# Three steps in fp32 products at the end of a sandwich kernel on one core, with the order behind the last scores written anew

## The reference

```python
def attn(x, weight_qkv, out_w, out_b):
    # q, k, v: a product whose low column bands are fp16, the middle band fp32
    q, k, v = split(mix_precision_matmul(x, weight_qkv))
    s = softmax(q / 16 @ k.T)
    return (s @ v) @ out_w.T + out_b

def ffn(x, W_r, W_k, W_v, mu_r, mu_k):
    x_prev = x shifted down by one row of its batch, zeros first
    xr = mu_r * x + (1 - mu_r) * x_prev
    xk = mu_k * x + (1 - mu_k) * x_prev
    r = sigmoid(xr @ W_r.T)
    k_act = relu(xk @ W_k.T) ** 2
    return r * (k_act @ W_v.T)

x = x + layernorm(attn(layernorm(x), ...))
x = x + layernorm(ffn(layernorm(x), ...))
```

## Time and profile before

| | |
|---|---|
| median of 3 runs | 807.6 us (807.54 to 808.79) |
| the profiled execution | 809.13 us, its span 807.3 us |
| TensorE busy | 784.2 us, 97% of the span |
| VectorE, ScalarE, POOL busy | 653.0 (81%), 576.7 (71%), 515.9 us (64%) |
| granted TensorE clock, mean | 0.993 |
| HBM read and written | 18.75 and 8.39 MB |

### The profile page before, as it was taken

The page is one execution under the profiler, slowest core; times in us unless marked ns, Lnnn a source line. Parts: engine busy times, 40 slices in busy tenths (PEclk is TensorE's granted clock), DMA queues, the critical chain, the costliest instruction groups (busy, mean ns, idle before and its releaser), DMA issues.

```text
span 807.3 us, 16567 instructions
## 1 busy us (share of the span) xinstructions
PE 784.2 (97%) x5839; PEld 574.0 (71%) x5839; DVE 653.0 (81%) x1681; ACT 576.7 (71%) x795; POOL 515.9 (64%) x752
## 2 busy tenths in 40 slices
PE   8999999999999999999999999999999999998983
PEld 6556777777777777777777777777777777777872
DVE  6788888877788979878888879978777788877876
ACT  4668668777777778877768687787767676675564
POOL 3340356765776868675676767876557657676674
PEclk9999999999999999999999999999999999999998
DMA  6788789577876768887666898857577766559301
GB/s 190 161 166 129 140 161 174 89 135 143 170 135 147 138 134 161 145 151 145 117 125 137 164 164 150 156 111 129 108 134 144 134 124 100 113 119 201 77 14 52
DMA packets 348243, 108.70 MB, mean 135 GB/s; under 512 B 321920, under 2 KB 347904, under 8 KB 348160
## 3 DMA queue, kind: packets, MB, share of 16 engines
q1 hardware_dynamic: 348160, 107.64, 69.6%
HBM read 18.75 MB, written 8.39 MB: 34 GB/s over the span
## 4 chain that ended last, share of the span: by engine, by line
PE 91%; DVE 3%; DMA 1%; issue 1%; POOL 1%; ACT 1%; POOLq 0%; DVEq 0%; ACTq 0%
PE Y L1492 7%; PE Y L1496 7%; PE Y L1493 7%; PE Y L1494 7%; PE Y L1495 7%; PE S L1471 7%; PE S L1475 7%; PE S L1474 7%; PE S L1473 7%; PE S L1472 7%; PE M L1436 6%; PE M L1438 6%; PE M L1437 6%; PE M L1453 1%; PE M L1451 1%
## 5 line engine op out<-in xcount | busy, mean ns | idle before, releaser
L1148 DVE TENSOR_SCALAR_CACHE_REDUCE probs<-S 128x512 f32<-128x512 f32 x256 | 172.9, 677 | 64.6 <-PE S L1475 64.4
L833 ACT ACTIVATE probs<-probs,exp_bias,kappa 128x2048 f32<-128x2048 f32 x64 | 133.9, 2092 | 64.2 <-DVE exp_bias L1161 64.2
L1166 DVE TENSOR_TENSOR p_lo<-probs,p_hi 128x2048 f16<-128x2048 f32 x62 | 171.5, 2767 | 7.3 <-ACT p_hi L762 7.3
L1493 PE MATMUL Y<-pt_lo,planes 128*128 128x256 f16 x496 | 135.2, 273 | 0.0
L1495 PE MATMUL Y<-pt_lo,planes 128*128 128x256 f16 x496 | 135.2, 273 | 0.0
L1494 PE MATMUL Y<-pt_hi,planes 128*128 128x256 f16 x496 | 135.2, 273 | 0.0
L1492 PE MATMUL Y<-pt_hi,planes 128*128 128x256 f16 x496 | 135.2, 273 | 0.0
L1496 PE MATMUL Y<-pt_hi,planes 128*128 128x256 f16 x496 | 135.2, 273 | 0.0
L762 ACT ACTIVATE p_hi<-probs 128x2048 f16<-128x2048 f32 x64 | 121.4, 1897 | 6.2 <-DMA pt_lo<-p_lo 6.1
L1471 PE MATMUL S<-turned,q_hi 128*128 128x512 f16 x256 | 97.1, 379 | 1.7 <-DVE probs L1148 0.9
L1475 PE MATMUL S<-turned,q_lo 128*128 128x512 f16 x256 | 97.0, 379 | 0.0
(11 more groups left out here) (223 smaller groups left out, 2032.6 us busy)
## 6 DMA issues: line engine op xcount, KB each, us to landing
x_res<-in_L_attn_x SPq DMA_DIRECT2D x32, 256.0 KB, 3.7
out_x<-gate SPq DMA_DIRECT2D x32, 256.0 KB, 3.2
xs<-in_L_attn_x SPq DMA_DIRECT2D x13, 512.0 KB, 4.7
pt_hi<-p_hi SPq DMA_TRANSPOSE x62, 5.0
pt_lo<-p_lo SPq DMA_TRANSPOSE x62, 4.8
xs<-in_L_attn_x SPq DMA_DIRECT2D x2, 256.0 KB, 4.0
gate<-in_L_attn_x SPq DMA_DIRECT2D x1, 512.0 KB, 6.8
att<-in_L_attn_x SPq DMA_DIRECT2D x1, 512.0 KB, 4.5
```

What stands on the lines that cost most here:

```text
L1148: dve.tensor_scalar(probs[:, h % 2, t, c * BLK:(c + 1) * BLK], S[k % RING][:, :], 1.0, None, ALU.mult, ALU.max, accum_out=chunk_max[:, t, ...
L1166: dve.tensor_tensor(p_lo[:, t, :], probs[:, h % 2, t, :], p_hi[:, t, :], ALU.subtract).then_inc(p_lo_made, 1)
L1493: pe.matmul(to[:, 0, :], low, p_l, start=False, stop=final, skip_group_check=True)
```

## The change

Steps 29, 30 and 31 (`h >= FULL`) no longer split. Their receptance, keys and feed are products of the fp32 tiles `mixed` and `square` with fp32 weights, which POOL makes once, in slots 218, 220 and 229, as the sum of the two planes (in tiles that batch 2 has left, `planes` and `turned`). An fp32 group is four products instead of 12. `split_high`, `split_low`, `sq_hi` and `squares_low` of these three steps are gone, and some waits name other semaphores (a mix of step 30 or 31 waits for the receptance or keys before it, no longer for the split). Behind the loop, the five lists by hand are in another order.

```diff
+    FULL = H - 3
+    FULL_AT = (218, 220, 229)
...
+        full = [f32(planes[:, 0].rearrange("p k l d -> p (k l d)")[:, NKT * ROWS:]).rearrange("p (w h c) -> p w h c", w=2, h=HALVES),
+                f32(turned[:, 0].rearrange("p k l d -> p (k l d)")[:, NKT * ROWS:]).rearrange("p (w h c) -> p w h c", w=2, h=HALVES)]
+        FULL_OF = {REC: full[0][:, 0], KEY: full[0][:, 1], VAL: full[1][:, 0]}
...
+            turn_low(H - 2, 1)
+            store(H - 8)
             turn_high(H - 2, 1)
-            turn_low(H - 2, 1)
-            load_residual(H - 3)
-            store(H - 8)
             turn_high(H - 1, 0)
...
+            def full_weight(w):
+                pool.wait_ge(pv_done, (NB - 1) * PER)
+                pool.tensor_tensor(FULL_OF[w], wt_hi[:, w], wt_lo[:, w], ALU.add).then_inc(full_made, 1)
...
             def squares(h):
                 act.wait_ge(key_done, h + 1)
-                if h >= LEFT:
+                if h > FULL:
+                    act.wait_ge(sq_made, h)
+                elif h >= LEFT:
                     act.wait_ge(sq_hi_made, h)
...
+                if h >= FULL:
+                    return
                 act.activation(sq_hi[:, :, :], relu[:, :, :], ACT.Square, scale=key_scale[:, 0:1]).then_inc(sq_hi_made, 1)
...
             def mix(h, i):
                 dve.wait_ge(diff_made, h + 1)
-                if h >= 1:
+                if h > FULL:
+                    dve.wait_ge(rec_done if i == 0 else key_done, h)
+                elif h >= 1:
                     dve.wait_ge(xm_lo_made[i], h)
...
+            def full_by_rows(to, a, w, done):
+                for t in range(RT):
+                    for e in range(HALVES):
+                        mm = pe.matmul(to[:, t * D:(t + 1) * D], a[:, e, t * P:(t + 1) * P], FULL_OF[w][:, e, :],
+                                       start=e == 0, stop=e == HALVES - 1)
+                mm.then_inc(done, 1)
...
             def receptance(h):
-                pe.wait_ge(xm_lo_made[0], h + 1)
+                if h >= FULL:
+                    pe.wait_ge(mixed_made[0], (h + 1) * HALVES)
+                    pe.wait_ge(full_made, 3)
+                else:
+                    pe.wait_ge(xm_lo_made[0], h + 1)
...
-            values(H - 3, 1, 2)
             project_out(H - 4, KEYS_LEFT)
-            values(H - 3, 2, 7)
+            values(H - 3, 1, 5)
+            mix_keys(H - 6, 0)
+            values(H - 3, 5, 8)
             receptance(H - 6)
             feed(H - 7)
             turn_mix_in(H - 5)
-            mix_keys(H - 6, 0)
-            values(H - 3, 7, 8)
             values(H - 2, 0, 3)
```

More of the change, by code:

```diff
@@ L483, in _ @@
             turn_low(H - 1, 1)
+            load_residual(H - 3)
+            store(H - 7)
             load_residual(H - 2)
-            store(H - 7)
+            load_residual(H - 1)
             store(H - 6)
-            load_residual(H - 1)
             store(H - 5)
@@ L1537, in receptance @@
                     pe.wait_ge(gated_made, h)
-                by_rows(REC_BANK, xm_hi[:, 0], xm_lo[:, 0], REC, rec_done)
+                if h >= FULL:
+                    full_by_rows(REC_BANK, mixed[:, 0], REC, rec_done)
+                else:
+                    by_rows(REC_BANK, xm_hi[:, 0], xm_lo[:, 0], REC, rec_done)
             def mix_keys(h, projects_begun):
-                pe.wait_ge(xm_lo_made[1], h + 1)
+                if h >= FULL:
+                    pe.wait_ge(mixed_made[1], (h + 1) * HALVES)
+                    pe.wait_ge(full_made, 3)
+                else:
+                    pe.wait_ge(xm_lo_made[1], h + 1)
                 if h >= KEYS_LEFT:
@@ L1548, in mix_keys @@
                     cols = slice(m * P, (m + 1) * P)
+                    if h >= FULL:
+                        for e in range(HALVES):
+                            mm = pe.matmul(pair(keys_bank(h)[:, :])[:, m, :], FULL_OF[KEY][:, e, cols], mixed[:, 1, e, :],
+                                           start=e == 0, stop=e == HALVES - 1)
+                        continue
                     for e in range(HALVES):
@@ L1560, in feed @@
                     pe.wait_ge(rec_made, h + 1)
-                by_rows(feed_bank(h), sq_hi, sq_lo, VAL, val_done)
+                if h >= FULL:
+                    full_by_rows(feed_bank(h), square, VAL, val_done)
+                else:
+                    by_rows(feed_bank(h), sq_hi, sq_lo, VAL, val_done)
             sources = [[stage_qkv[e][:, w * D:(w + 1) * D] for e in range(HALVES)] for w in range(3)]
@@ L1647, in _ @@
             turn_mix_in(H - 5)
-            mix_keys(H - 6, 0)
-            values(H - 3, 7, 8)
             values(H - 2, 0, 3)
+            project_out(H - 3, KEYS_LEFT)
+            turn_mix_in(H - 4)
             feed(H - 6)
-            project_out(H - 3, KEYS_LEFT)
-            values(H - 2, 3, 4)
+            values(H - 2, 3, 8)
             mix_keys(H - 5, 0)
-            values(H - 2, 4, 8)
-            turn_mix_in(H - 4)
-            values(H - 1, 0, 1)
+            values(H - 1, 0, 2)
+            project_out(H - 2, KEYS_LEFT)
+            values(H - 1, 2, 6)
+            turn_mix_in(H - 3)
+            feed(H - 5)
+            values(H - 1, 6, 8)
             receptance(H - 5)
-            project_out(H - 2, KEYS_LEFT)
-            feed(H - 5)
-            values(H - 1, 1, 3)
             mix_keys(H - 4, 0)
-            turn_mix_in(H - 3)
-            values(H - 1, 3, 8)
-            feed(H - 4)
             project_out(H - 1, KEYS_LEFT)
@@ L1669, in _ @@
             mix_keys(H - 3, 0)
+            feed(H - 4)
             receptance(H - 3)
@@ L1672, in _ @@
             mix_keys(H - 2, 0)
+            receptance(H - 2)
             turn_mix_in(H - 1)
-            receptance(H - 2)
             feed(H - 2)
```

164 lines of the change are left out of this document (78 added, 86 removed).

## The result

| | before | with the change |
|---|---|---|
| median of 4 runs each, taken together | 808.19 us (807.54 to 809.2) | 802.88 us (802.23 to 803.22) |
| ratio to before | | 0.9929, 95% interval 0.9916 to 0.9943 |
| the profiled execution | 809.13 us, span 807.3 | 803.22 us, span 801.4 |
| granted TensorE clock, mean | 0.993 | 0.998 |

The change makes the kernel 5.3 us faster by the medians and 5.9 by the spans of the profiled executions. The two differ since the profiled execution of before lies 0.9 us above its median and that of the change 0.3. The forecast was a gain of 8.1: 799.5 us, in a range of 797.2 to 803.5 that holds 802.88, if near its end. Of the 3.4 us between 799.5 and 802.88, 0.6 are the base (807.6 when the forecast was made, 808.19 with all runs) and 2.8 are gain that did not come.

A forecast was written before the change was run, and what follows sets the result against it. TensorE products bound the loop; behind it 15.4 us are lost to stops and lower clock. Less 1.5 of waits, 4.7 of fp32 work and 1.1 for handovers, the gain is 8.1 us: 799.5 us, range 797.2 to 803.5.

The forecast's parts named there:

- The bound: TensorE is full inside the loop; the stretch behind it holds all there is to gain, 15.4 us lost.
- Sums of planes hidden: Three weight-plane sums on POOL, about 615 to 648 us in the loop, cost nothing; at most 4.8 us.
- Rival C: Sums of weight planes on POOL delay the loop: 4.8 us back, 804.3 us; chance 0.03.
- The first stop, 1.0 us before project_out(28): Behind the loop, TensorE newly waits 1.0 us for y_lo, since a unit of values no longer stands ahead.
- +4.7 us for nine fp32 groups: Steps 29 to 31: nine groups of four fp32 products take 1.83 instead of 1.31 us each, 4.7 more.
- The stop before receptance(26) goes: Behind the loop, the 2.59 us stop before 738.16 and the lower clock behind it go; operand ready 736.9, wanted 738.9.
- Those two waits and 1.1 us for handovers: TensorE's only waits behind the loop: 1.0 before project_out(28), 0.5 before keys(31); plus 1.1 us for semaphore handovers.
- The walk: Tracing five engine queues from 727.55 us, with durations from the trace; last products end at 791.4.
- the allowance: 1.1 us taken off the gain for semaphore handovers behind the loop, with ends of 0 and 4.
- the prediction's own sum (9.2): Gain behind the loop before handovers: 15.4 lost, less 1.5 of waits and 4.7 of added work, 9.2 us.
- rival A: A stop returns before turn(28), POOL's norm late beside VectorE's p_lo, then lower clock: price 3.6, 803.1 us; chance 0.15.
- Rival B: fp32 products from keys(29) to feed(31) run at the lower clock, 1.83 us more per group, up to 816.0; chance 0.06.

The follow-up runs named there:

- The short sums: The changed kernel with three of POOL's sums cut to two columns, so it also does less work: 801.44 us, ratio 0.9906 to before.
- the ScalarE order: The changed kernel with ScalarE's squares, receptance and turned rows of steps 26 and 27 ahead of step 28's second norm: 801.47 us, ratio 0.9907 to before.

## Why the prediction was right, and where it fell short

- **The bound.** Right: all of the gain lies behind the loop, 66.32 us instead of 72.85, and the clock there is 1.00.
- **Sums of planes hidden.** Right: POOL +4.1 us in 610 to 660, TensorE busy all of it. Rival C is out.
- **The first stop, 1.0 us before project_out(28).** Right as a stop, 1.05. But it was booked as a loss that stands by itself, and the run with a unit of values in front shows that without it turn(28) and project_out(29) wait instead.
- **+4.7 us for nine fp32 groups.** Measured: six groups take 1.73 and three 1.80 to 1.83, 15.8 instead of nine times 1.31, so +4.1. My 1.83 came from a group that stood behind a gap; those groups are recorded as 1.99 us, the others as 1.89. My 0.229 was the mean of seven unequal distances: in that group, as in keys(31), the second record starts 0.32 us behind the first, and the others 0.216 apart. The estimate from the Trainium skill ("FP8 and Floating Point Precision", TensorE Precision Notes), 1.71, is what groups in sequence take within 0.02, and I was wrong to let that one row decide against it. Why the first product behind a wait takes 0.1 more is open.
- **The stop before receptance(26) goes.** Right, and with it the lower clock behind it. With fp32 products in the old order it stays (2.57), so it is the order's doing.
- **"Those two waits and 1.1 us for handovers."** This is the step that failed. The walk gave TensorE 1.5 us of waits, and it has 4.3. Of those missing, 1.04 is turn(28), where the walk had it 0.1 us from waiting, and 1.45 are receptance(30) and turn(31), where it had 0.9 and 1.2 to spare; the other 0.3 is keys(31), 0.76 instead of 0.5. But for one meeting of POOL with p_lo, the durations that I gave VectorE and POOL were those of rows without a neighbour. On the changed kernel's last chain three of VectorE's are 0.7 to 0.8 longer each, and ahead of turn(28) POOL meets p_lo twice (2.14 and 2.38 us). The short sums show the first; the ScalarE order shows that the second need not have cost anything. The trace of before had such rows, and the walk took 0.85 for a mix all the same: four mixes take 2.49 in the earlier trace rows, and a pair of them took 1.80 beside POOL's sum (the rows stand below this list). Also, the walk had no time from the last feed to the gating (0.3 us).
- **The sum again, with what was measured:** 8.1 - 2.8 (waits) + 0.6 (fp32 groups) + 1.1 (the allowance, now in the waits) - 0.5 (where the tail starts) - 0.3 (last handover) gives 6.2, beside 5.9 of the spans; the 0.3 left is as large as the distance at which the prediction's own sum (9.2) and its walk (800.33 less 791.4, or 8.9) stood from the start.
- **The range.** It held partly by luck: the groups booked 0.6 us too dear and the allowance of 1.1 covered 1.7 of the 2.8 us of waits that the walk lacked, and of the mechanism behind turn(28) the forecast had only the 0.15 of rival A.
- **Rival A.** Its mechanism came: small POOL operations beside p_lo delayed turn(28), if not the square root itself, which took 0.69, but the shift of the first norm and the operation ahead of the second root. Its price didn't: 1.04 us, and no lower clock behind it, instead of 3.6.
- **Rival B.** Not in the changed kernel. In the old order, where a stop of 2.96 stands ahead of an fp32 receptance, it cost 1.0 us.

The pair of mixes and POOL's sum in the trace of before (timeline of VectorE, then of POOL):

```profile
745.00 1.80 DVE L1223 SCALAR_TENSOR_TENSOR mixed<-diff,mu,xt 128x256 f32<-128x256 f32 x2 [0.33 <-POOL diff L654]
...
744.92 1.59 POOL L629 TENSOR_TENSOR res<-x_res,att 128x256 f32<-128x256 f32 x2
```

## What to carry to other kernels

One fp32 product in place of three fp16 ones costs TensorE time and takes the splits off the chain that feeds it; it pays at the end of a pipeline, where TensorE waits for splits, and the queues should be ordered anew for it: here the products alone gave about half of the gain, and the order without them a loss. When such a tail is walked, take VectorE's and POOL's durations from rows where both work side by side, and give every chain with less than a microsecond to spare a wait of its own. Before buying off a stop, look which operand is next and whether it comes by another chain: three of the reorderings here moved a wait instead of removing it.

## What was not expected of the hardware

- VectorE's fp32 norm of two times 256 columns took 0.73 us alone and 1.44 beside POOL's difference, a mix 0.88 and 1.58; POOL's operation on 128x2 took 2.38 beside a p_lo of 2.29.
- The fp32 group of four takes 1.73 us in sequence and 1.83 behind a wait, and the 0.1 lies in its first record.
- The length of a stop alone doesn't tell whether the granted clock falls. In the kernel with planes in the new order it was 1.00 from 783 to 787 us, behind a stop of 3.09, and 0.70 from 790 to 794, behind one of 3.41:

```profile
783.00:787.00 4.00, 2.79 (x24) 2.26 (x24) 2.54 (x9) 1.49 (x4) 3.62 (x8) 1.00 0.01 2
...
790.00:794.00 4.00, 4.00 (x28) 3.18 (x25) 0.91 (x4) 1.07 (x3) 2.08 (x5) 0.70 0.13 44
```

In the changed kernel, whose stops are at most 1.05 us, it never fell behind the loop.
